# A macaron block on one core: fetches paced by other points, denominators summed on GpSimd, two batches' queries rounded on ScalarE

## The reference, cut to what matters

```python
x = x + 0.5 * ffn(layernorm(x))     # round one (r = 0)
x = x + attn(layernorm(x))
x = x + 0.5 * ffn(layernorm(x))     # round two (r = 1)
```

```python
agg = sum_k(exp(clip(q . ky / sqrt(8), -15, 15))) + EPS
w   = log(1 + (abs(q . k / sqrt(8)) + EPS) / (agg + EPS))
out = sum_k(w * v) / (sum_k(w) + EPS)
```

## Time and profile before

| | us |
|---|---|
| median of 3 runs | 424.56 |
| lowest, highest | 424.08, 425.61 |
| the profiled execution | 427.45 |
| its span, first to last instruction | 425.5 |

### The profile page before, as it was taken

One profiled execution on the slowest core, in us unless ns is written; L12 is line 12 of the kernel. 1 busy time (PEld: TensorE's weight loads), 2 busy tenths in 40 slices (PEclk: granted clock), 3 DMA queues, 4 the chain that ended last, 5 costly groups with the idle time before them and its releaser, 6 DMA issues.

```text
span 425.5 us, 8298 instructions
## 1 busy us (share of the span) xinstructions
PE 322.0 (76%) x2376; PEld 194.2 (46%) x2376; DVE 311.7 (73%) x667; ACT 296.7 (70%) x862; POOL 143.4 (34%) x230
## 2 busy tenths in 40 slices
PE   6868999636776545768778597776978977899992
PEld 6627899513143211323323133232333464588991
DVE  5763443367879989999999999998999557543431
ACT  2814556414989999999999979997677655245561
POOL 7164555500334470024020241202530012654543
PEclk9989999958689755886978869699899976999997
DMA  8584766133477998003000030000300273567540
GB/s 248 210 267 125 204 172 165 62 99 127 131 203 204 224 236 163 0 2 99 2 0 2 0 87 13 3 0 2 99 2 2 69 269 108 166 189 195 163 132 31
DMA packets 37992, 47.60 MB, mean 112 GB/s; under 512 B 4288, under 2 KB 26816, under 8 KB 37696
## 3 DMA queue, kind: packets, MB, share of 16 engines
q1 hardware_dynamic: 33616, 36.20, 32.1%
q0 software_dynamic: 2560, 6.30, 4.9%
q10 hardware_dynamic: 1776, 4.60, 3.1%
HBM read 24.02 MB, written 6.29 MB: 71 GB/s over the span
## 4 chain that ended last, share of the span: by engine, by line
PE 36%; ACT 26%; DVE 17%; issue 9%; DMA 6%; POOL 2%; SPq 2%; DVEq 0%; POOLq 0%; ACTq 0%
ACT R L896 11%; PE PS L1436 10%; PE PS L1446 8%; ACT R L904 7%; ACT CL L896 5%; DVE R L1237 5%; PE PS L1579 4%; DVE R L1222 3%; PE PS L1371 2%; DMA R<-rows_d,R 2%; DVE CL L1222 2%; PE PS L1362 2%; PE PS L1561 2%; PE PS L1592 2%; SPq L467 1%
## 5 line engine op out<-in xcount | busy, mean ns | idle before, releaser
L1237 DVE TENSOR_TENSOR R<-PS,MB 128x1024 int32<-128x1024 int32 (+1 forms) x96 | 97.9, 1036 | 7.3 <-PE PS L1561 7.1
L791 ACT ACTIVATE R<-PS,R 128x128 f32<-128x128 f32 x184 | 52.4, 368 | 51.2 <-PE PS L1436 26.8
L904 ACT ACTIVATE R<-R 128x1024 f32<-128x1024 f32 x64 | 80.1, 1261 | 8.7 <-DVE R L1237 8.5
L896 ACT ACTIVATE R<-R 128x384 f32<-128x384 f32 (+2 forms) x192 | 77.1, 407 | 5.0 <-DVE R L1222 4.9
L1546 PE MATMUL PS<-R 64*128 64x512 bf16 (+3 forms) x256 | 39.9, 365 | 32.6 <-DVE CL L1222 15.5
L1579 PE MATMUL PS<-R,V 128*32 128x256 f32 (+3 forms) x512 | 56.4, 527 | 6.7 <-ACT R L904 6.5
L1222 DVE SCALAR_TENSOR_TENSOR R<-PS,MA 128x1024 f32<-128x1024 f32 x64 | 59.7, 948 | 0.9 <-PE PS L1546 0.7
L1436 PE MATMUL PS<-R 128*128 (+1 forms) x368 | 51.4, 283 | 5.0 <-DVE R L1107 2.5
L1446 PE MATMUL PS<-R 128*128 (+1 forms) x368 | 48.8, 276 | 0.7 <-ACT R L791 0.7
L1436 PEld LDWEIGHTS PS<-R 128*128 128x128 f32 x368 | 44.6, 191 | 8.7 <-issue 5.6
L1561 PE MATMUL PS<-QPS,R 64*128 64x512 bf16 (+3 forms) x256 | 38.0, 348 | 13.8 <-DVE R L1222 10.2
(11 more groups left out here) (168 smaller groups left out, 462.7 us busy)
## 6 DMA issues: line engine op xcount, KB each, us to landing
R<-w SPq DMA_DIRECT2D x38, 258.0 KB
R<-R SPq DMA_DIRECT2D x32, 128.0 KB, 2.4
R<-R SPq DMA_DIRECT2D x16, 256.0 KB, 7.1
QPS<-R SPq DMA_DIRECT2D x32, 128.0 KB, 2.5
R<-w ACTq DMA_DIRECT2D x8, 258.0 KB
rows_d<-X SPq DMA_DIRECT2D x8, 256.0 KB, 3.9
R<-w ACTq DMA_DIRECT2D x1, 2048.0 KB, 9.5
rows_d<-R SPq DMA_DIRECT2D x8, 256.0 KB, 2.3
```

The lines of the kernel that those rows point to most:

```text
L791: last = act.activation(HT[:, k % 2, c * P:(c + 1) * P], PS[:, k % 2, c * P:(c + 1) * P], ACT.Gelu, bias=W1[:, k, F + c:F + c + 1])
L896: act.activation(e, e, ACT.Exp, scale=SCALE, accum_out=aggf[:, ds(s + (2 * i + par) * STEPS, 1)])\
L904: act.activation(w, w, ACT.Ln, bias=1.0, scale=1.0).then_inc(s_ln, 1)
L1237: dve.tensor_tensor(weights(v)[:, :, at:at + n].bitcast(i32), PS[:, SLOTS[slot(b_fill(v, g))], 0:n].bitcast(i32), spread(mask, 1, 2), ALU. ...
```

## The change

- `fetch_in_slot`: tiles 4 to 15 wait for other points, mostly of the slot before the one they waited for. Tiles 8 and 12 wait for VectorE's copy of a transpose (s_vx) in place of a down product (s_dn).
- `scatter_back`: the wait for the down product of the next slot is gone.
- Denominators of batches 0 to 2: GpSimd adds the summed weights ahead of the numerators (s_den), and VectorE takes the reciprocal behind group 0 of step at = 22. The last batch stays as it was.
- Batches 1 and 2 (MIDDLE): ScalarE rounds the scaled queries in the step after Q_AT, between the first log piece and the exponentials, and VectorE subtracts behind group 1 of that step.
- Batch 0: the residual stands behind group 0 of the step after X_AT, the moments behind group 1.

```diff
--- before.py
+++ after.py
@@ -29,8 +29,6 @@
 RING = 4
 FETCHED, FASTER = 4, 7
-LATER = 12
 NS = NT + E - 1
 H, HD = 16, 8
 HP = H // 2
@@ -93,6 +91,8 @@
 LN_EARLY = (NB - 1) * HP + N_AT
 TURN_AT = ((NB - 1) * HP + Q_AT + 8, (NB - 1) * HP + Q_AT + 9, STEPS + LAG - 1, (NB - 1) * HP + X_AT)
+MIDDLE = (1, 2)
 ROUTE_TILES = ((0, 8), (8, 16)), ((0, 8), (8, 16))
 SCORE_BANKS, RANK_BANKS, INDEX_BANK, COEF_BANK = ((2, 3), (3, 2)), ((4, 5), (5, 4)), 2, 3
@@ -347,7 +347,8 @@
         s_pool = sem("pool_chain")
         s_apre = sem("agg_sums_ready")
         s_arec = sem("agg_reciprocals_ready")
-        s_dpre = sem("denominator_part_ready")
+        s_dpre = sem("last_denominator_part_ready")
+        s_den = sem("denominators_summed")
         s_drec = sem("denominator_reciprocal_ready")
         s_ck = sem("ck_ready")
         s_vp = sem("v_prefix_scaled")
@@ -564,21 +565,24 @@
                 n, k = divmod(t - FASTER, 4)
-                if t < FASTER:
-                    pool.wait_ge(s_up, r * NS + t - FETCHED + 1)
+                if t == FETCHED:
+                    pool.wait_ge(s_px, r * NT + 1)
+                elif t < FASTER:
+                    pool.wait_ge(s_up, r * NS + t - FETCHED)
                 elif k == 0:
-                    pool.wait_ge(s_y, r * NS + 3 * n + 2)
+                    pool.wait_ge(s_y, r * NS + 3 * n + 1)
                 elif k == 1:
-                    pool.wait_ge(s_dn, r * NS + 3 * n + 3)
+                    pool.wait_ge(s_vx, r * NT + 3 * n + 4)
                 elif k == 2:
-                    pool.wait_ge(s_px, r * NT + 3 * n + 6)
+                    pool.wait_ge(s_px, r * NT + 3 * n + 5)
                 else:
-                    pool.wait_ge(s_up, r * NS + 3 * n + 6)
+                    pool.wait_ge(s_up, r * NS + 3 * n + 5)
             def gather(r):
                 pool.wait_ge(s_src, r + 1)
@@ -594,9 +598,6 @@
                 for t in range(NT):
                     pool.wait_ge(s_y, r * NS + t + E)
-                    if t <= LATER:
-                        pool.wait_ge(s_dn, r * NS + t + E + 1)
                     to = bass.IndirectOffsetOnAxis(source[:, t:t + 1], 0)
                     if r == 0:
                         pool.indirect_dma_start(x_d, to, XS[:, t, P:2 * P], None).then_inc(s_xd, 16)
@@ -686,7 +687,10 @@
                 seen_h = spread(seen[:, :].rearrange("p (n o) -> p n o", o=1), 2, H)
                 link(pool.tensor_tensor(den.rearrange("p (i h) -> p i h", i=TB), ck[:, b % 2, :, :],
                                         seen_h, ALU.mult))
-                pool.tensor_scalar(den, den, EPS, None, ALU.add).then_inc(s_dpre, 1)
+                if b == NB - 1:
+                    pool.tensor_scalar(den, den, EPS, None, ALU.add).then_inc(s_dpre, 1)
+                else:
+                    link(pool.tensor_scalar(den, den, EPS, None, ALU.add))
             def scaled_q_terms(b):
@@ -707,10 +711,12 @@
                     pool.tensor_tensor(numf, numf, aof[:, :, 0:HD], ALU.add).then_inc(s_sum, 1)
                     return
+                den = rt[:, 5, :]
+                pool.tensor_tensor(den, den, aof[:, :, HD], ALU.add).then_inc(s_den, 1)
                 link(pool.tensor_tensor(numf, numf, aof[:, :, 0:HD], ALU.add))
                 pool.wait_ge(s_drec, b + 1)
-                pool.tensor_tensor(numf, numf, spread(rt[:, 5, :].rearrange("p (n o) -> p n o", o=1),
-                                                      2, HD), ALU.mult).then_inc(s_num, 1)
+                pool.tensor_tensor(numf, numf, spread(den.rearrange("p (n o) -> p n o", o=1), 2, HD),
+                                   ALU.mult).then_inc(s_num, 1)
             for s in range(END_STEP):
                 for b in range(NB):
@@ -903,6 +909,12 @@
                 w = weights(v)[:, :, (0, SEQ)[part]:(SEQ, HEAD_W)[part]]
                 act.activation(w, w, ACT.Ln, bias=1.0, scale=1.0).then_inc(s_ln, 1)
+            def scaled_q(b):
+                act.wait_ge(s_qt, b + 1)
+                act.wait_ge(s_qps, STACK_DMAS * b)
+                act.activation(QP3[:, 0, :], PS[:, 7, :], ACT.Copy).then_inc(s_qhi, 1)
             def av_out(v):
                 act.wait_ge(s_av, TB * (v // 2 + 1))
@@ -926,6 +938,9 @@
                     exponentials(s - 1, 2)
                 if 0 <= v < STEPS:
                     logs(v, 0)
+                for b in MIDDLE:
+                    if s - b * HP == Q_AT + 1:
+                        scaled_q(b)
                 if s < STEPS:
                     exponentials(s, 0)
                     exponentials(s, 1)
@@ -1264,10 +1279,12 @@
             def scaled_q_terms(b):
-                dve.wait_ge(s_qt, b + 1)
-                if b:
-                    dve.wait_ge(s_qps, STACK_DMAS * b)
-                dve.tensor_copy(QP3[:, 0, :], PS[:, 7, :]).then_inc(s_qhi, 1)
+                if b not in MIDDLE:
+                    dve.wait_ge(s_qt, b + 1)
+                    if b:
+                        dve.wait_ge(s_qps, STACK_DMAS * b)
+                    dve.tensor_copy(QP3[:, 0, :], PS[:, 7, :]).then_inc(s_qhi, 1)
                 dve.wait_ge(s_qhi, b + 1)
                 dve.tensor_tensor(QREM, PS[:, 7, :], QP3[:, 0, :], ALU.subtract).then_inc(s_qrem, 1)
@@ -1279,7 +1296,7 @@
                         dve.wait_ge(s_apre, b + 1)
                         dve.reciprocal(rt[:, 0:2, :], rt[:, 0:2, :]).then_inc(s_arec, 1)
-                    if at == Q_AT:
+                    if at == Q_AT and b not in MIDDLE:
                         scaled_q_terms(b)
                 m = s - 1 + FIRST_PROJECTIONS
                 if s == 1:
@@ -1297,27 +1314,44 @@
                     at = s - b * HP
                     if at == V_AT:
                         v_prefix(b)
-                    if at == N_AT:
-                        dve.wait_ge(s_dpre, b + 1)
-                        dve.wait_ge(s_ao, HP * (b + 1))
+                    if b == NB - 1 and at == N_AT:
+                        dve.wait_ge(s_dpre, 1)
+                        dve.wait_ge(s_ao, HP * NB)
                         den = rt[:, 5, :]
                         link(dve.tensor_tensor(den, den, AO.rearrange("p i h c -> p (i h) c")[:, :, HD],
                                                ALU.add))
                         dve.reciprocal(den, den).then_inc(s_drec, 1)
-                        if b == NB - 1:
-                            numf = NUM.rearrange("p i h c -> p (i h) c")
-                            dve.wait_ge(s_sum, 1)
-                            dve.wait_ge(s_drec, NB)
-                            dve.tensor_tensor(numf, numf, over_e(den, HD), ALU.mult).then_inc(s_num, 1)
-                    if at == X_AT:
-                        dve.wait_ge(s_pr, b + 1)
-                        xb = X[:, b * TB:(b + 1) * TB, :]
-                        dve.tensor_tensor(xb, PS[:, 7, :].rearrange("p (n d) -> p n d", n=TB), xb,
-                                          ALU.add).then_inc(s_xr, 1)
-                        dve.wait_ge(s_xr, b + 1)
+                        numf = NUM.rearrange("p i h c -> p (i h) c")
+                        dve.wait_ge(s_sum, 1)
+                        dve.wait_ge(s_drec, NB)
+                        dve.tensor_tensor(numf, numf, over_e(den, HD), ALU.mult).then_inc(s_num, 1)
+                    if b and at == X_AT:
+                        residual(b)
                         moments(b)
+            def residual(b):
+                dve.wait_ge(s_pr, b + 1)
+                xb = X[:, b * TB:(b + 1) * TB, :]
+                dve.tensor_tensor(xb, PS[:, 7, :].rearrange("p (n d) -> p n d", n=TB), xb,
+                                  ALU.add).then_inc(s_xr, 1)
+                dve.wait_ge(s_xr, b + 1)
+            def between(s, g):
+                for b in range(NB):
+                    at = s - b * HP
+                    if g == 0 and at == N_AT + 1 and b < NB - 1:
+                        dve.wait_ge(s_den, b + 1)
+                        dve.reciprocal(rt[:, 5, :], rt[:, 5, :]).then_inc(s_drec, 1)
+                    if b == 0 and at == X_AT + 1:
+                        if g == 0:
+                            residual(b)
+                        if g == 1:
+                            moments(b)
+                    if b in MIDDLE and g == 1 and at == Q_AT + 1:
+                        scaled_q_terms(b)
             for s in range(END_STEP):
                 v = s - LAG
@@ -1331,6 +1365,7 @@
                         heads_out(leaving(v))
                     if s < STEPS:
                         clip_scores(s, g)
+                    between(s, g)
                 after(s)
                 if s == LN_EARLY - 1:
                     variance(4)
```

## The result

The changed kernel takes 421.63 us, the median of 20 runs (419.81 to 425.55), against 424.79 us for the kernel before in the same session (20 runs, 422.00 to 428.08). The ratio is 0.9932, with a 95% interval of 0.9911 to 0.9953: 2.9 us or 0.7% faster (the two medians themselves lie 3.2 us apart). Forecast were 5.8 us. The sign and the range held; the size was half.

A forecast was written before the change was run, and what follows sets the result against it. VectorE and ScalarE, both nearly full, bound attention until 288 us, then TensorE leads. The terms 3.6 - 0.3 + 1.8 + 0.6 + 0.1 = 5.8 us gave 418.8 us from 424.56, range 415.5 to 423.0.

The forecast's parts named there:

- Attention: forecast 3.6 us: Attention stage: ScalarE's idle time shrinks by 4.6 us, less 1.0 for two added copies; bounds 1.0 and 5.1.
- (d): Attention, batches 1 and 2: queries subtracted 3.8 us later, transfers end at 205.8, scores at 205.7; cost 0, bounds 0 to 1 each.
- the carrying forward of lead and idle: Attention from 194.81 us: VectorE's lead and ScalarE's idle computed step by step from both engines' rates, giving 3.6 us.
- The five idles: Attention: ScalarE's idle times of 1.4, 0.7, 1.6, 1.7, 0.7 (6.1 us) become 0, 0, 0.5, 0.6, 0.4 (1.5).
- the prediction's formula: Attention: ScalarE's idle is 0.30 minus VectorE's lead in opening the step, or -0.18 minus lead with the extra copy.
- rival 2: Attention: VectorE gets ahead, then waits for TensorE's scores or late stacks; 1.0 of 3.6 us stays, about 423 us; chance 0.15.
- Denominators of batch 2: After 288 us: GpSimd's extra add lies in the chain TensorE waits for; costs 0.3 us, bounds -0.4 and +0.6.
- Fetches: Feed-forward rounds: tile 13's fetch no longer queued behind tile 12's, saving 0.9 us twice, 1.8 us; bounds 0 and 3.5.
- late slot 6 of both rounds: Feed-forward rounds: VectorE idled 1.54 and 1.57 us before the same slot's result, beside a queued fetch; 0.6 us expected after.
- Rival 1: Feed-forward rounds: late starts are not due to fetches and stay; only attention and last store gain, 4.0 us, 420.5; chance 0.28.
- Stores: Feed-forward rounds: stores leave with their row; last one 0.6 us after it instead of 1.22, saving 0.6, round one 0.1.
- Rival 3: Feed-forward rounds: fetches and stores at the new point stall transpose copies 0.7 us each, up to 430 us; chance 0.06.

The follow-up runs named there:

- fewer_weighed_products: The changed kernel with half of the value products of head pairs 2 to 19 left out; ratio 0.9926 to the kernel before, on chip C.
- fetches_at_once: The changed kernel with no fetch waiting for anything, all 16 one behind the other; ratio 0.9940 to the kernel before, on chip C.
- change_again: The changed kernel once more without an edit; ratio 0.9996 to the kernel before, on chip A.
- fetches_only: The kernel before with only the fetches on their new points, the stores as before; ratio 1.0057 to the kernel before, on chip A.
- attention_only: The changed kernel with the old fetch points and the old wait of the stores; ratio 0.9964 to the kernel before, on chip A.
- attention_again: The changed kernel with old fetch points and old stores' wait, run on chip C; ratio 0.9962 to the kernel before.

## Why the prediction was half right

**Attention: forecast 3.6 us, measured 2.4.** The median of the stage is 124.8 us over six traces without the attention part and 122.4 over nine with all of it (122.2 without fewer_weighed_products). The two groups do not overlap (124.28 to 127.27, 121.43 to 123.10). By the times the attention part alone is worth less, 1.5 us on A (0.9964, an interval that just takes in 1) and 1.6 on C (0.9962), with intervals that hold the traces' figure too. The mechanism was right. ScalarE's named waits fell from 4.6 us to 2.5, the copy costs 0.47 and the 0.96 us add went. No score waited for the stack, as (d) had it, but by 0.7 us: the transfers ended when forecast (205.8 in the time of before is 203.0 here, the opening of ScalarE's step 18 being 2.8 us earlier), while the scores came 1.0 us later than (d) had them. Without the shortfall that follows they would have come at 202.9, just ahead of the last transfer, so this term held by a narrow margin.

What failed is the carrying forward of lead and idle. From the step at 18 to that at 32 ScalarE took 91.82 us instead of the forecast 89.97. The five idles, forecast 0, 0, 0.5, 0.6 and 0.4, are 0.6, 0.4, 0.6, 1.05 and 0.6, and another gap of 0.15 is left. The recurrence let VectorE open a step as early as its own work allowed. The trace shows that it can't: where the 1.3 us of query work went away, VectorE reached the scores first and stopped, for 0.18, 0.24 and 0.48 us around step 18 and for 0.37 us in the step of batch 2's queries. That work had covered the time that TensorE takes to deliver. So VectorE opened step 18 at 192.17, 0.20 us behind ScalarE and not 0.25 ahead. The lost lead is missing later too: it opens step 22 at 217.59, 0.34 us ahead of ScalarE's 217.93, and with the reciprocal's 0.46 the prediction's formula gives 0.30 - 0.34 + 0.46 = 0.42 us of idle, where none was forecast and 0.43 was measured. This is rival 2 in its first half. By the medians it took 1.2 of the 3.6 us (1.85 in this one trace), less than the 2.6 at which I bounded it.

Why TensorE delivered late is argued and not tested. At both places it works without a gap, at the lower level of its clock, with 1.9 us of value products ahead of the scores. The clock itself did not change (0.66 in 187 to 197 us after and 0.66 in 190 to 200 before); at this level it may be what sets how early VectorE can go on. fewer_weighed_products was to test this and left TensorE's time nearly as it was.

**Denominators of batch 2: forecast -0.3.** From the end of the attention window to round two's first result the median went from 85.8 to 86.1 us over the same traces. The size agrees, but single traces run from 84.3 to 87.4 us, so that this neither shows nor refutes the term.

**Fetches: forecast 1.8 us, measured nothing on chip C and a loss on chip A.** This is the term that failed whole. It read the late slot 6 of both rounds as a matter of where a fetch stood beside another. On chip A late results come 1.2 to 1.9 us after the start of a fetch or store that stands close behind another, as before's 51.02 came after 49.40. But more than half of those were not queued, and removing the queued one moved the late result to another slot. On chip C no pacing has a late result, and on chip B the new one has none, the only one that ran there. The profile of before (44.85 and 44.87 us, slot 6 late) looks like chip A's old pacing (44.91 and 44.83); the profile of after looks like B and C, and on C the old pacing too gives 43.01 and 42.49. So the 4.0 us that the profiles seem to show in the rounds are put down to the chip. That is an inference: on which chip each of the two profiles was taken is not recorded. But the timed executions, 2.9 us apart, have no room for 4.0 us beside what attention and the last store gained. Rival 1 had this right: 5.8 - 1.8 = 4.0 us.

The Trainium skill, page SBUF — State Buffer, section "SBUF: two separate sides", says that VectorE and GpSimd exclude each other only at a shared port, which VectorE wants in its two-port modes or with two SBUF inputs. By that rule the add, which reads the products from PSUM, is not held by a fetch. fetches_at_once on C agrees (0.42 and 0.50 us of idle beside back-to-back fetches). The 1.54 us on A is not explained by that rule either, since in change_again ScalarE, which the page has outside the shared port, started at the same moment as VectorE (40.22 and 40.20).

**Stores: forecast 0.6 at the end and 0.1 in round one.** The last store follows its row by 0.63 us after 1.22, the forecast to 0.03. Each trace without the stores' wait has it on all three chips (0.62 to 0.63), and fetches_only, attention_only and attention_again, which keep the wait, have 1.18 to 1.22. The 0.1 was too small to see.

The terms from the traces are 2.4 - 0.3 + 0.6 = 2.7 us, against 2.9 timed, with the 0.3 taken as forecast. Rival 1 less 1.2 us for VectorE's stops is 4.0 - 1.2 = 2.8. That so close a sum comes out is in part luck, since the single terms are known to half a microsecond or worse. Rival 3, the slower case, had a real core: on chip A 9 of the 12 rounds with the new fetch points take 46.0 to 47.1 us and 3 take 44.8 to 45.1, against 44.9 with the old ones, though not by the 8 stalls that it named.

## What to carry to other kernels

Before a gap in one trace is priced as something the code can remove, see whether the same kernel shows it in a second trace: here it came and went with the chip, and two profiles taken apart told 7.4 us where the times told 2.9. When two engines run side by side nearly full, work taken from ahead of a step frees only as much as the third engine's next delivery is early; carry that arrival along in the recurrence, not only the two engines' own rates. When an experiment takes work from an engine, look in its trace whether time went with it: here half the products went and the time stayed. Time each part of a change alone, since a part that costs may hide behind one that pays.

## What the runs showed of the hardware that was not expected

- The same kernel takes 1.1% longer on one chip than on the others (429.7 against 425.1 to 425.3 us), and 1.9 us of that lies in each feed-forward round (44.91 against 43.01 us with the old pacing, 44.83 against 42.49 in the second round, there 2.3). The clock is not the reason: the changed kernel was granted 0.835 on A (change_again) and 0.834 on C (change_third). In time the changed kernel is 430.3 us on A and 422.1 on C.
- On chip A alone of the three, VectorE now and then starts a slot's result 1.2 to 1.9 us after the start of a fetch or store of GpSimd that came 1.25 to 2.0 us behind another. In the two places looked at, in change_again and attention_only, ScalarE starts within 0.08 us of VectorE. TensorE had gone on with its products (at 39.40 us in change_again). What differs between the chips stays open.
- An indirect fetch of 128 rows occupies GpSimd for 0.94 to 0.99 us, and one queued behind another starts 1.25 us after it.
- TensorE's value products took the same time with half of them left out: 1.92 us for 4 against 1.94 for 8 at a clock of 0.50, 0.84 against 0.85 for the 128x384 ones (fewer_weighed_products and after).
